# A cross-attention and expert-routing kernel: weighted sum moved ahead of the next query, turned output ahead of the next scores, and VectorE's order behind the last tile

## The reference, cut to what matters

```python
q = layernorm(x) @ wq.T + bq;  K = ctx @ wk.T + bk;  V = ctx @ wv.T + bv
scores = einsum('bhqd,bhkd->bhqk', Qh, Kh) / 4       # causal and key masks -> -inf
out = einsum('bhqk,bhkd->bhqd', softmax(scores), Vh)
x = x + tanh(g_xattn) * (out @ wo.T + bo)
z = layernorm(x); logits = z @ Wr + br
gates, idx = max and argmax of softmax(logits)       # 8 experts, one for each token
h = relu(ln(z) @ W1[idx] + b1[idx]); y = (h @ W2[idx] + b2[idx]) * gates
x = x + tanh(g_ffn) * y
```

## Time and profile before

| | |
|---|---|
| time, median of 3 runs | 278.11 us (276.93, 278.11, 278.54) |
| the profiled execution, its own time | 278.49 us |
| its span, first to last instruction | 276.7 us |
| TensorE busy | 268.3 us, 97% of the span |
| VectorE busy | 201.5 us, 73% |
| ScalarE busy | 166.3 us, 60% |
| GpSimd busy | 131.9 us, 48% |

### The profile page before, as it was taken

One profiled execution on the slowest core, in us unless ns is written; L12 is line 12 of the kernel. 1 busy time (PEld: TensorE's weight loads), 2 busy tenths in 40 slices (PEclk: granted clock), 3 DMA queues, 4 the chain that ended last, 5 costly groups with the idle time before them and its releaser, 6 DMA issues.

```text
span 276.7 us, 7230 instructions
## 1 busy us (share of the span) xinstructions
PE 268.3 (97%) x2310; PEld 238.7 (86%) x2310; DVE 201.5 (73%) x687; ACT 166.3 (60%) x444; POOL 131.9 (48%) x255
## 2 busy tenths in 40 slices
PE   8999999999999999999999999999999999999993
PEld 4879899999899999988899799899878799988992
DVE  6699479888888888899679966985547545543564
ACT  2435467777677777676776655795438445453551
POOL 3444146677877778644775424432322042222421
PEclk9999799999999999999999999999999999999998
DMA  7999998010112464565343131412201122120222
GB/s 213 257 307 374 372 376 286 5 38 39 41 40 52 191 191 186 189 195 190 116 118 118 48 104 48 129 50 80 60 23 46 49 63 61 61 57 27 59 60 61
DMA packets 19948, 34.42 MB, mean 124 GB/s; under 512 B 2392, under 2 KB 14486, under 8 KB 19899
## 3 DMA queue, kind: packets, MB, share of 16 engines
q1 hardware_dynamic: 15945, 22.33, 24.8%
q0 software_dynamic: 3808, 11.42, 13.3%
q10 hardware_dynamic: 146, 0.07, 0.1%
HBM read 27.45 MB, written 6.75 MB: 124 GB/s over the span
## 4 chain that ended last, share of the span: by engine, by line
PE 80%; DVE 8%; issue 6%; POOL 3%; DMA 2%; DVEq 0%; POOLq 0%
PE pS L1897 17%; PE pB L1671 12%; PE pB L1967 9%; PE pT L1582 7%; PE pB L1689 7%; PE pA L1582 5%; PE pB L1972 4%; PE pS L1625 4%; PE pA L1605 3%; PE pT L1605 2%; PE pT L1699 2%; POOL out_dram L473 1%; POOL zin L456 1%; DMA W2s<-in_ctx_dram 1%; DVE hA L1346 1%
## 5 line engine op out<-in xcount | busy, mean ns | idle before, releaser
L1897 PE MATMUL pS<-znf,W1c 128*128 128x128 f32 x576 | 71.0, 276 | 0.3 <-DVE ticks L1334 0.3
L1897 PEld LDWEIGHTS pS<-znf,W1c 128*128 128x128 f32 x576 | 67.2, 192 | 3.0 <-issue 2.9
L473 POOL DMA_INDIRECT out_dram<-yo,idxs x17 | 17.2, 1010 | 76.4 <-DVE yo L1377 72.4
L1967 PE MATMUL pB<-W2p,hT 128*128 128x512 f32 x136 | 38.9, 408 | 0.5 <-DVE ticks L1386 0.4
L761 ACT ACTIVATE hA<-pS,b1s 128x128 f32<-128x128 f32 x72 | 20.5, 367 | 30.5 <-PE pS L1897 24.9
L1346 DVE TENSOR_SCALAR hA<-pS,b1s 128x128 f32<-128x128 f32 x72 | 20.2, 344 | 20.3 <-PE pS L1897 19.9
L621 ACT ACTIVATE Pb<-Pb 128x616 f32<-128x616 f32 x32 | 23.0, 718 | 15.4 <-DVE Pb L931 15.4
L772 ACT ACTIVATE hT<-hA 128x512 fp32r<-128x512 f32 x36 | 22.9, 640 | 14.5 <-DVE hA L1346 14.5
L1967 PEld LDWEIGHTS pB<-W2p,hT 128*128 128x128 f32 x136 | 23.0, 188 | 5.9 <-issue 2.1
L923 DVE TENSOR_REDUCE mx<-pS 128x8 f32<-128x616 f32 x32 | 25.3, 789 | 1.8 <-PE pS L1629 1.8
L456 POOL DMA_INDIRECT zin<-rows_dram,idxg x21 | 22.1, 1051 | 9.5 <-issue 5.3
(11 more groups left out here) (282 smaller groups left out, 546.6 us busy)
## 6 DMA issues: line engine op xcount, KB each, us to landing
W1s<-in_L_ffn_W_dram SPq DMA_DIRECT2D x8, 1024.0 KB, 10.8
W2s<-in_L_ffn_W_dram SPq DMA_DIRECT2D x8, 1024.0 KB, 11.4
rows_dram<-pay POOLq DMA_DIRECT2D x12, 260.0 KB, 3.9
xs<-in_x_dram SPq DMA_DIRECT2D x3, 512.0 KB, 8.6
rows_dram<-pay SPq DMA_DIRECT2D x4, 260.0 KB, 2.0
W2s<-in_sel_dram SPq DMA_DIRECT2D x1, 385.0 KB
zin<-rows_dram,idxg POOLq DMA_INDIRECT x21, 3.7
out_dram<-yo,idxs POOLq DMA_INDIRECT x17
```

The lines of the kernel that those rows point to most:

```text
L1897: t = e.matmul(pS[:, 2 * (s % 2) + n, 128 * c:128 * c + 128], W1c[k][n][:, 128 * c:128 * c + 128], znf[s % 2][:, 128 * k:128 * k + 128], s ...
L1967: e.matmul(o2, hT[s % 2][0][:, 128 * c:128 * c + 128], W2p[c // 2][:, :, D * (c % 2):D * (c % 2) + D], start=False, stop=True, skip_group_ ...
```

## The change

It does four things.

1. TensorE: all ten chunks of `attend(n-1)` stand ahead of `query(n+1)`. `transpose_O(n-1)` stands at the end of iteration n, ahead of `scores(n+1)`; before, it stood behind those scores.
2. The other engines follow: VectorE takes the three steps of `norm(n-1)` earlier in the iteration, among the statistics and ahead of `normed1(n+2)`, in every iteration but the last; ScalarE's `copy_OT(n-1)` stands behind `query(n+1)`, and `z_row(n-3)` ahead of the second exponential.
3. VectorE behind the last tile: the remaining steps of `rank(1)` (four instructions of L1090) stand behind `W1_copies(1)` where they were mixed into `stats2(z)`; `out_rows_of(0)` and `relu(1)` stand behind the tables `R` and behind `W2_lows(1)`.
4. `WARM[0]` is 7 where it was 6.

```diff
-WARM = (6, 3, 2)
+WARM = (7, 3, 2)
@@ ScalarE
             for n in range(NT):
-                if n >= 2:
-                    copy_OT(n - 2)
...
                     copy_PT(n - 1, 2)
+                    if n >= 3:
+                        z_row(n - 3)
                     exp(n, 1)
...
                     query(n + 1)
-                if n >= 3:
-                    z_row(n - 3)
+                if 2 <= n < NT - 1:
+                    copy_OT(n - 1)
...
                     e.activation(boR[:, :], bank["T1"][:, 16:24], ACT.Copy, scale=tg[:, 0:1]).then_inc(g["act_wT"], 1)
+                    copy_OT(0)
@@ VectorE, the loop
                 next(routed, None)
+                if n < NT - 1:
+                    next(normal, None)
                 next(x_stats, None)
+                if n < NT - 1:
+                    next(normal, None)
                 table_steps(3)
                 next(routed, None)
+                if n < NT - 1:
+                    next(normal, None)
                 if n + 2 < NT:
                     normed1(n + 2)
@@ VectorE, behind the last tile
             resid(z)
-            together(stats2(z), ranked_here)
+            together(stats2(z))
             W1_copies(1)
+            together(ranked_here)
...
-            out_rows_of(0)
             e.wait_ge(g["dve_own"], t_s)
             for hf in range(2):
...
-            relu(1)
-            W2_lows(1)
-            new_expert(3)
             e.wait_ge(g["dve_own"], t_cs)
             e.tensor_reduce(ef[:, KA:NS], cs, AX.X, ALU.add).then_inc(g["dve_own"], 1)
             t_ef = own.up()
+            W2_lows(1)
+            out_rows_of(0)
+            relu(1)
+            new_expert(3)
             e.wait_ge(g["pe_ids"], 2)
@@ TensorE
                 scores(n)
                 if n >= 2:
-                    transpose_O(n - 2)
                     transpose_P(n - 1, 0)
                     project(n - 2)
...
-                    attend(n - 1, range(8 if n > 1 else NC))
+                    attend(n - 1)
...
                     query(n + 1)
-                if n > 1:
-                    attend(n - 1, range(8, NC))
...
                 if n:
                     route(n)
+                if 1 <= n < NT - 1:
+                    transpose_O(n - 1)
```

More of the change, by code:

```diff
@@ L1658, in transpose_P, with attend @@
                 t.then_inc(g["pe_PT"], 1)
-            def attend(i, chunks=range(NC)):
+            def attend(i):
                 b = i // TPB
@@ L1663, in attend @@
                     e.wait_ge(g["dve_VB"], 2)
-                for c in chunks:
+                for c in range(NC):
                     n = chunk_rows(c)
@@ L1672, in attend @@
                                  stop=(c == NC - 1), skip_group_check=True)
-                if c == NC - 1:
-                    t.then_inc(g["pe_PV"], 1)
+                t.then_inc(g["pe_PV"], 1)
             def transpose_O(i):
```

## The result

The changed kernel is slower: 281.44 us (median of 5 runs, 281.15 to 288.71), where the kernel before took 277.64 us in the same session. The ratio is 1.0138, with a 95% interval of 1.0085 to 1.019. I had forecast 276.3.

What follows compares the result with a forecast made beforehand. TensorE was taken to set the loop's period, VectorE the chain behind the last tile; -2.5 + 0.25 + 0.34 + 0 + 0.07 = -1.8 us, so 276.3 us for the median, with 274.8 to 277.9 holding eight in ten.

Steps and rivals of the forecast that it cites:

- The loop, -2.5: Iterations 3 to 13: TensorE's lost waits give 0.23 us a tile, 11 tiles, 2.5 us less (2.2 to 2.9).
- The projection's wait: Loop, TensorE before the projection: 0.20 us lost waiting for ScalarE's copy of the turned output; it leaves, no other follows there.
- Counted from the start of the scores: the weighted sum began at 3.53 ... less 0.29 and 0.20, plus 0.06, that is 3.1.: Loop, checking `On` is early enough: the weighted sum would begin 3.1 us behind the scores' start; `On` has 0.3 us slack.
- All ten chunks take 1.73 + 0.38 = 2.11: Loop, TensorE: the whole weighted sum takes 2.11 us, so the query begins at 5.2 us from the scores' start.
- The query's second copy ... lies under the router's product and the two transposes, 0.7 together.: Loop, ScalarE: the copy starts 0.04 us behind its matmul, takes 0.37, and is covered by 0.7 us of TensorE's work.
- rival (d): Loop: the wait moves to the transposes of `On` or the probabilities' copy; 278.8 us at worst, 277.5 with half; chance 0.18.
- Iteration 14, +0.25: VectorE, bound by the tables, stands at L940 waiting for the later weighted sum; 0.25 us more (0 to 0.4).
- W1_copies(1), +0.34: VectorE behind the last tile: instructions no longer cover the branch's cost, so one more gap of 0.34 us (0 to +0.6).
- Output and relu, 0: Behind the last tile: TensorE starts `output(1)` earlier but stands 1 us before its second group; 0 (-0.1 to +0.2).
- The seventh dummy, +0.07: At the start: a seventh dummy occupies TensorE from 3.63 to 4.06, past the first real matmul's start; 0.07 us more.
- Rival (a): At the start: the seventh dummy brings the higher clock sooner, giving back 0.9 us, 275.4 us; chance 0.12.
- Rival (e): Loop: VectorE becomes the bound, holding everything behind L940; period 7.3 us, 281.0 us in all; chance 0.07.

Runs made afterwards that it cites:

- e6: e5 with one small VectorE step, the second gate step, moved from ahead of `resid` to behind it; 279.07 us, 0.9991 of the kernel before.
- e8: The kernel before with the whole weighted sum ahead of the query and nothing else; period 7.27 us, ratio 1.0083.
- e10: e7 with ScalarE's `x2_row` of a tile moved next to its `z_row` in the following iteration; 275.98 us, 0.9943 of the kernel before.
- e17: e10 with six dummies and VectorE's old order behind the last tile; 278.15 us, 1.0008 of the kernel before.
- e13: The kernel before, nothing of the change, with both repairs of e10 (maxima and probabilities order, row's copy moved); ratio 1.0101, period 7.09 us.
- e5: The changed kernel with VectorE making the router's remaining steps ahead of the steps of `norm` in iteration 13; 280.12 us, 1.0044 of the kernel before.
- e9: The changed kernel with six dummy matmuls ahead of the ranks in iteration 13, the wait kept; 281.09 us, 1.0069 of the kernel before.
- e2: The kernel before with VectorE's order behind the last tile alone changed; ratio 1.000.
- e15: The kernel before with only ScalarE's copy of the row's second half (`x2_row`) moved next to that of its first half; ratio 1.0114.
- e7: e5 with both maxima first, then `resid`, then both subtractions, and ScalarE copying turned probabilities ahead of the first exponential; 279.31 us, 0.9989 of the kernel before.
- e12: e5 with the weighted sum split again, its last two chunks behind the query; period 7.94 us, 1.0371 of the kernel before.
- e1: The kernel before with the loop's order alone changed, on all engines; 281.84, 281.92, 287.21 and 287.65 us.

## Why the prediction was wrong, point by point

**The loop, -2.5: wrong, and it is the step that failed.** The projection's wait did go, as I had read it. I held that 0.23 us a tile followed, because I looked for the next late thing in two places only, `On` and VectorE's total, and both were in time. Of the steps as the prediction put them, these don't hold:

- "Counted from the start of the scores: the weighted sum began at 3.53 ... less 0.29 and 0.20, plus 0.06, that is 3.1." It began at 3.19 (91.96 less 88.77), since `resid` holds its bank. In iteration 14 I had seen this very wait; in the other tiles I never counted `resid`'s end from the scores: maximum at 0.88, three steps, 0.42 for itself, 3.04, and 0.15 until the sum.
- "All ten chunks take 1.73 + 0.38 = 2.11": in one row they took 2.24 (94.20 less 91.96). The kernel before has them in one row in iteration 15, with the same 2.24 (127.36 to the router's product at 129.60).
- "The query's second copy ... lies under the router's product and the two transposes, 0.7 together." From the start of the router's product these gave 0.58 (0.36 and two of 0.11), and the copy starts 0.20 behind it, takes 0.37, and the scores come 0.14 later, 0.71.

These come to 0.09, 0.13 and 0.13. The router's product gave 0.14 of it back (0.36 for the 0.50 that I took), and what is left, 0.21, is nearly all of my 0.23. This is rival (d), "the wait only moves", with other destinations than the two that it named. e6 shows the first of them and e8 what the third costs when it grows; the second is only read from the rows. Mended (e10, e17), the order is worth 0.14 us a tile, 60% of my term, and e13 shows that the repairs without the change give none of it.

I also took the exceptional iterations for common ones or for nothing: iteration 1 pays 0.27 us for the order, iteration 4 0.19 and iteration 8 0.13.

**What I put at nothing: the ranks, +1.4, and 1.0 for the clock.** I asked who waits for what is queued behind L940 and named `transpose_x` and GpSimd's sum. In iteration 13 it is also `ranks(0)`, through the router's one-hot row. e5 and e9 show both halves. Next to the loop's own term this is the largest error, and the rule by which I worked (name who waits for everything that is queued) would have found it, had I gone through it iteration by iteration.

**Iteration 14, +0.25: the right sign, too small.** At the full clock it took 7.60 us (e9), for 7.15 before: +0.45, beyond my 0 to 0.4. **Iteration 15**, for which I took nothing, has a wait of 0.82 us ahead of its sum, but the sum begins only 0.10 later than before (3.76 us behind the scores for 3.66).

**W1_copies(1), +0.34: wrong in kind.** e2 shows none of it. I took the gap of the earlier trace rows for the price of the branch, because no wait was named; it was VectorE's wait for `hidden(0, 1)`, and the chain that I read as running on VectorE "with no rest" passes through TensorE there. The Trainium skill, "Advanced Engine Details and Errata", section Control Flow Timing, gives a compare-and-branch about 108 ns. e2 shows no more than that: the marker starts 0.08 us behind the end of the statistic ahead of the branch (140.94), and the next instruction 0.02 behind the marker's start.

**Output and relu, 0: right** by the start of the second group (0.02 us later), and so was where TensorE would stand instead, though for 0.67 us and not 1. **The seventh dummy, +0.07: not measurable** (1.0011). Rival (a), the earlier clock, was there in the profile of after and would have misled: six dummies have it too.

**Rival (e)** did not happen: the maxima start 0.88 us behind their scores, for 0.91 before. The slower side came in through a wait, not through VectorE's total.

## What to carry to other kernels

When a wait leaves a loop whose period repeats to 0.01 us, follow the new order once around, from the scores of one tile to those of the next, through each engine, and compare the longest closed chain with the sum of the bounding engine's work: the time won here was given back in two places, neither of which waited before. An in-order queue that is made to wait earlier must be gone through for every iteration that differs from the common one, since its late consumers (here the ranks) show up in only one of sixteen. And a semaphore that paces transfers is part of the order too: a copy moved by half an iteration sent the last 1 MB load into the first gather, in e15, which lost 3.2 us. Last, a gap that the profile lays to "issue" may be a wait all the same: compare its distance from the producer in a second trace before giving it a cause.

## What the runs showed of the hardware that I had not expected

In after and in e7, an idle stretch of TensorE (1.34 and 0.53 us) is followed by several microseconds in which part runs at the lower of the two levels, 1.2 in place of 2.4 GHz, and behind the first of them that costs 1.0 us, nearly as much as the stretch itself. With six dummies in its place (e9) the granted clock stayed 1.00 up to 124 us. Yet in e12 TensorE stands 0.67 us in every tile and the granted clock is 1.00 from 100 to 132 us, and in the kernel before it is 0.68 in 28 to 32 us, in which TensorE is busy for all 4.00. The Trainium skill, "TensorE: Matmul & The Clock Gate", Part 1, says that the clock follows recent activity; after, e7 and e9 agree, and what sets e12 and that stretch apart stays open.

The executions of one kernel differ by their low stretches: e10 took 275.1 us at a granted clock of 0.998 and more and 277.4 at 0.986, the kernel before in the same session 275.4 and 275.7 in its two best of 29. At such clocks, then, e10 is 0.3 to 0.6 us ahead. Its loop gains more than that, 1.15 us by the starts of scores(4) and scores(15), 78.06 us for 79.21. But iterations 0 and 1 take 17.28 us together for 16.73, half of it from the change's order and half from the repairs (17.01 in e1, 17.00 in e13). How much of the 0.6% is that the clock stays up more often is not shown.
